# Second layer's attention: value matmuls of two steps issued together, every second step

## The chip, the cores and the metric

The kernel runs on one core of one Trainium2 chip. The metric is the device time of one launch in microseconds (us). Five engines work side by side from instruction queues of their own and meet through semaphores: TensorE (PE in the profile; its weight loads are PEld), VectorE (DVE), ScalarE (ACT), GpSimd (POOL) and SyncE (SP, which here only issues DMAs).

## The reference, cut to what matters

Two layers of attention and feed-forward work on 2048 tokens of width 128. The change touches only the last block, an attention with 8 heads in which each head's query, key and value come from five experts with gates:

```
q5 = (x @ Wq).reshape(b, t, H, E, DH)             # H=8, E=5, DH=64
kv = (x @ Wkv).reshape(b, t, 2, H, E, DH)
q = einsum('bthed,bthe->bhtd', q5, sd_g)          # gates: the top 3 of 5 experts
k = einsum('bthed,bthe->bhtd', k5, ss_g)
v = einsum('bthed,bthe->bhtd', v5, ss_g)
attn = softmax(einsum('bhid,bhjd->bhij', q * scale, k))
out = einsum('bhij,bhjd->bihd', attn, v)
o5 = einsum('bthd,dm->bthm', out, Wo)...; x + einsum('bthem,bthe->btm', o5, md)
```

## The kernel before

Everything stays in on-chip memory. The last block goes through 8 heads (`h`), each through 4 chunks (`c`) of 512 queries, each chunk through `M1` = 8 steps of 256 keys: 32 steps (`U1`) a head, 256 in all, numbered `u`. One list, `SEQ1`, sets the order of work on every engine: `merge` puts a step's foreground (`foreground1`) between background items (`preparation1`) that have due times in steps, and each engine walks the list and does its own part of each item. For a step `u` the foreground items are:

- `S`: the scores of step `u`, 4 full-width matmuls on PE (L775, L776) into two of four PSUM banks; ACT then takes their exponential (L960) into one of five buffers `pbuf1`.
- `V` (L786): the value product of a step, on PE, for the step two before. Each of two key tiles of 128 gives 64 output rows; the first tile uses columns 0 to 63 of the array and the second 64 to 127 (`tile_position=(0, 64 * i)`). Both add up in PSUM bank `ACC`. Each fp32 matmul is two records in the trace, so a `V` has four.
- `D`: the running denominator of that same step, an addition of the exponentials, the first 704 of 1024 columns on DVE (L1280 the first time, L1283 after that), the rest on POOL (L1383).
- `O`: every 8 steps ACT copies the sum out of `ACC`; `F`: two steps after it PE folds the two halves and sums the denominators (L797, L802), DVE divides (L1291, L1292), POOL applies the expert mask and adds into `z` (L1394, L1398).

The background, for the head that comes next, is `proj` (48 a head, three fp32 matmuls each, L747 to L749, read by DVE with the gates at L1238 and summed over the experts by POOL), `t` and `q2` (transposes, L581, read by ACT), and `max` (64 a head, one matmul of 512 columns, L759, read by a row maximum on DVE, L1256). A cast of the next head's weights (`w`, L1230 and L1231, on DVE) comes once a head.

All results of `proj`, `max`, `t`, `q2` and `F` go through a ring of three PSUM banks. In PE's code, `take` waits until the reader of the item three turns earlier in the ring is done:

```
turn = ring.turn[step]
if turn >= len(RING):
    wait_read(pe, ring, ring.order[turn - len(RING)])
return ring.bank(step)
```

The foreground of the second half of a step, before the change:

```
if 0 <= u - 2 < U1 * H1:
    seq += [("V", u - 2), ("D", u - 2)]
```

Within a head, steps 2 to 19 carry the `proj` items (2 or 3 a step, with about 2 `max`); steps 20 to 31 and 0 to 1 carry `max` (1 to 3 a step) and the last transposes. The last head has no `proj`.

Of the kernel before, what the change touches and what calls it, by code (L numbers as in the profile page):

```python
# [32 lines left out]
D = 128  # L33
# [125 lines left out]
def build(nc, A):  # L159
    ctx = ExitStack()  # L160
    with ctx:
# [211 lines left out]
        def foreground1(u, half):  # L373
            if half == 0:
                return [("S", u)] if u < U1 * H1 else []
            seq = []
            if 0 <= u - 2 < U1 * H1:
                seq += [("V", u - 2), ("D", u - 2)]
                if (u - 1) % M1 == 0:
                    seq.append(("O", (u - 1) // M1 - 1))  # L380
            if 0 <= u - 4 < U1 * H1 and (u - 3) % M1 == 0:
                seq.append(("F", (u - 3) // M1 - 1))
            return seq
# [6 lines left out]
        for c in range(NC):  # L390
            u = 2 * (N0 * (NG - 1) + LAST0[c] + 3) + 1
# [9 lines left out]
        for n in range(NT):  # L401
            u = U1 * (H1 - 1) + M1 * (n // TPC + 1) + 3
# [6 lines left out]
        assert [s for s in SEQ0 if s[0] in ("pj", "mix")] == [  # L409
            ({"sd": "pj", "sd2": "mix"}[s[0]], s[1]) for s in NORM if s[0] != "sd3"]  # L410
        SEQ1 = merge(by_place(preparation1() + after1), U1 * H1 + 16, foreground1)
        ring0 = Ring(SEQ0, ("max", "F", "pj", "mix", "lin"), ("k", "q", "q2", "at", "lt", "lt2"))
        ring1 = Ring(SEQ1, ("proj", "max", "F", "y"), ("t", "q2", "zt"))
# [1033 lines left out]
```

## Time and profile before

| what | value |
| --- | --- |
| median of 3 runs | 1856.27 us (1856.07 to 1857.29) |
| profiled execution, span | 1857.2 us |
| PE busy | 1645.3 us, 89% |
| DVE busy | 1435.4 us, 77% |
| POOL busy | 878.0 us, 47% |
| ACT busy | 782.5 us, 42% |

The only time shown of the profiled execution is its span, from its first to its last instruction. It lies 0.9 us over the median of the runs, so what lies around the span is taken as nothing. The 256 steps of the last block run from 796.6 us to about 1833 us of it. "Busy" of PE is the union of the matmul records; a record lasts longer than the time until the next one can start, so gaps are best read from the starts.

### The profile page before, as it was taken

The page shows a single profiled execution, that of the slowest core. Times are in us where ns is not written, and L with a number is a line of the kernel's source. Part 1 is how long each engine was busy: PE and PEld are TensorE (multiplying, and loading weights), DVE is VectorE, ACT ScalarE, POOL GpSimd, SP SyncE. Part 2 cuts the span into 40 slices and gives each one's busy share as a digit, 9 for nine tenths or more (in the row PEclk, how much of TensorE's full clock was granted, in tenths as well). Part 3 has the DMA queues.
Part 4 walks back from the last instruction along what each step waited for, and adds up shares of the span by engine and source line. Part 5 has one row for each costly group of instructions (what it writes and reads, how often), then busy time and mean ns, then how long its engine had stood idle before and what let it go on. Part 6 is the DMA issues. An engine that isn't in the chain of part 4 may idle for free.

```text
span 1857.2 us, 26270 instructions
## 1 busy us (share of the span) xinstructions
PE 1645.3 (89%) x8612; PEld 999.3 (54%) x8612; DVE 1435.4 (77%) x2387; ACT 782.5 (42%) x1046; POOL 878.0 (47%) x906
## 2 busy tenths in 40 slices
PE   3899999999999672699899899899999899899997
PEld 2555555555554361566466466466565565565554
DVE  4996785785786369888888888888898888988862
ACT  3457557567556320223433434334334234234441
POOL 2710000000000024358678589589588587687654
PEclk9799999999999775889899999999999999999996
DMA  2000000000000000000000000000000000000000
GB/s 58 1 1 1 1 1 1 1 1 1 1 1 1 11 1 11 0 11 1 11 1 2 11 1 1 11 1 1 12 1 1 11 1 1 1 1 1 1 11 13
DMA packets 12224, 9.34 MB, mean 5 GB/s; under 512 B 3840, under 2 KB 11584, under 8 KB 12096
## 3 DMA queue, kind: packets, MB, share of 16 engines
q1 hardware_dynamic: 12096, 7.66, 1.5%
q8 instruction: 77, 1.26, 0.3%
q14 instruction: 51, 0.42, 0.1%
HBM read 6.61 MB, written 1.05 MB: 4 GB/s over the span
## 4 chain that ended last, share of the span: by engine, by line
PE 66%; DVE 19%; issue 7%; POOL 5%; ACT 2%; SPq 0%; DMA 0%; DVEq 0%; POOLq 0%; ACTq 0%
PE ps L786 10%; PE ps L606 8%; PE ps L623 7%; PE ps L638 7%; PE ps L759 6%; PE ps L581 5%; PE ps L775 4%; PE ps L776 4%; DVE den L1283 3%; PE ps L747 3%; DVE mxp L1256 3%; PE ps L749 2%; PE ps L748 2%; POOL z L1398 2%; PE ps L797 2%
## 5 line engine op out<-in xcount | busy, mean ns | idle before, releaser
L960 ACT ACTIVATE pbuf<-ps 128x1024 f32<-128x1024 f32 x256 | 262.1, 1024 | 524.0 <-PE ps L776 520.9
L1074 DVE TENSOR_REDUCE mxp<-ps 128x1 f32<-128x512 f32 (+3 forms) x560 | 354.2, 671 | 112.2 <-PE ps L606 56.2
L1256 DVE TENSOR_REDUCE mxp<-ps 128x1 f32<-128x512 f32 x512 | 342.5, 682 | 66.8 <-PE ps L759 66.1
L875 ACT ACTIVATE pbuf<-ps 128x1024 f32<-128x1024 f32 (+3 forms) x320 | 281.7, 896 | 199.1 <-PE ps L626 98.5
L1283 DVE TENSOR_TENSOR den<-den,pbuf 128x704 f32<-128x704 f32 x224 | 292.0, 1303 | 1.1
L786 PE MATMUL ps<-pbuf,h_v 128*64 128x512 f32 x1024 | 284.4, 634 | 0.0
L759 PE MATMUL ps<-k1T,q1T 128*128 128x512 f32 x512 | 223.4, 453 | 38.7 <-DVE mxp L1256 25.1
L1383 POOL TENSOR_TENSOR den<-den,pbuf 128x320 f32<-128x320 f32 x224 | 235.0, 1049 | 42.1 <-ACT pbuf L960 26.5
L606 PE MATMUL ps<-kM,qT 128*128 128x512 f32 (+3 forms) x640 | 243.6, 427 | 9.5 <-ACT kM L862 4.3
L1238 DVE TENSOR_TENSOR gt<-ps,gate 128x320 f32<-128x320 f32 x384 | 182.6, 484 | 54.8 <-PE ps L749 51.7
L623 PE MATMUL ps<-qT,kM 128*128 128x512 f32 (+3 forms) x640 | 207.7, 399 | 8.4 <-ACT pbuf L875 8.4
L775 PE MATMUL ps<-q1T,k1T 128*128 128x512 f32 x512 | 209.4, 409 | 2.3 <-ACT q2T L950 2.3
L776 PE MATMUL ps<-q2T,k2T 65*128 65x512 f32 x512 | 204.6, 400 | 0.0
L606 PEld LDWEIGHTS ps<-kM,qT 128*128 128x128 f32 x640 | 122.4, 197 | 118.7 <-DVE mxp L1074 88.7
L747 PE MATMUL ps<-wh,xh 128*128 128x320 f32 x384 | 136.1, 355 | 53.5 <-DVE gt L1238 36.9
L1367 POOL TENSOR_TENSOR gs<-gt 128x384 f32<-128x384 f32 x120 | 148.3, 1236 | 67.0 <-DVE gt L1238 65.3
L759 PEld LDWEIGHTS ps<-k1T,q1T 128*128 128x128 f32 x512 | 98.8, 194 | 146.3 <-DVE mxp L1256 87.0
L638 PE MATMUL ps<-pbuf,stagev 128*32 128x512 f32 (+3 forms) x1280 | 152.0, 547 | 0.0
L747 PEld LDWEIGHTS ps<-wh,xh 128*128 128x128 f32 x384 | 73.5, 191 | 142.1 <-DVE gt L1238 68.7
L1325 POOL TENSOR_SCALAR rstd<-meanvar 128x4 f32<-128x4 f32 x12 | 2.7, 227 | 304.5 <-DVE meanvar L995 304.5
L1340 POOL COPY stagev<-qkv 128x512 f32<-128x512 f32 x4 | 2.9, 722 | 288.8 <-PE ps L638 266.1
L623 PEld LDWEIGHTS ps<-qT,kM 128*128 128x128 f32 x640 | 117.9, 195 | 35.4 <-ACT pbuf L875 22.9
(212 smaller groups left out, 2484.3 us busy)
## 6 DMA issues: line engine op xcount, KB each, us to landing
wraw<-in_Wkv SPq DMA_DIRECT2D x16, 160.0 KB, 2.6
wraw<-in_Wq SPq DMA_DIRECT2D x8, 160.0 KB, 2.3
out<-x SPq DMA_DIRECT2D x4, 256.0 KB, 2.3
wqkv<-in_wqkvT SPq DMA_DIRECT2D x1, 192.0 KB, 4.0
masks<-in_masks SPq DMA_DIRECT2D x1, 128.0 KB, 4.1
dft<-in_dft SPq DMA_DIRECT2D x1, 128.0 KB, 2.3
wout<-in_Wo SPq DMA_DIRECT2D x2, 64.0 KB, 2.6
ident<-in_ident SPq DMA_DIRECT2D x1, 64.0 KB, 5.7
```

What stands on the lines that cost most here:

```text
L606: mm = pe.matmul(ps[:, bank, w * a:w * (a + 1)], qT[:, g % 2, P * it:P * (it + 1)], kM[g % 2][:, h + a, CH * b:CH * b + w], start=True, st ...
L623: mm = pe.matmul(ps[:, b, off:CH], kM[g % 2][:, h, P * jt:P * (jt + 1)], qT[:, g % 2, CH * c + off:CH * (c + 1)], start=True, stop=jt < TP ...
L638: mm = pe.matmul(ps[32 * h:32 * h + 32, ACC, off:CH], stagev[:, g % 2, jt, h, :], pbuf0[:, u % NP0, h % 2, off:CH], start=jt == 0, stop=jt ...
L747: pe.matmul(o, xh[:, t], wh[:, j, :], start=True, stop=False)
L759: pe.matmul(ps[:, bank, :], q1T[:, h % 2, P * it:P * (it + 1)], k1T[:, h % 2, CH * b:CH * (b + 1)], start=True, stop=True).then_inc(s_turn ...
L775: pe.matmul(ps[:, b, :], k1T[:, h % 2, t], q1T[:, h % 2, q], start=True, stop=False)
L776: mm = pe.matmul(ps[:, b, :], k2T[0:D1 + 1, h % 2, t], q2T[0:D1 + 1, h % 2, q], start=False, stop=True)
L786: mm = pe.matmul(ps[64 * i:64 * i + 64, ACC, :], h_v[:, h % 2, 2 * m + i, :], pbuf1[:, u % NP1, i, :], start=m == 0, stop=m == M1 - 1, til ...
L875: nc.scalar.activation(pbuf0[:, u % NP0, :, off:CH], ps[:, b:b + 2, off:CH], ACT.Exp, scale=float(D0) ** -0.5).then_inc(s_exp, 1)
L1074: v.tensor_reduce(mxp[:, i, h:h + n, b], ps[:, ring0.bank(step), 0:w * n].rearrange("p (h k) -> p h k", h=n), AX.X, ALU.max).then_inc(s_re ...
L1256: v.tensor_reduce(mxp1[:, it % TPC, b:b + 1], ps[:, ring1.bank(step), :], AX.X, ALU.max).then_inc(s_read1d, 1)
L1283: v.tensor_tensor(dn, dn, w, ALU.add).then_inc(s_den1, 1)
```

## The change

The `V` of an even step is no longer issued two steps later, but together with that of the following odd step: in every odd step `u`, `V` of `u - 3` and `V` of `u - 2` stand one behind the other. In even steps only `D` stands there. `D`, `O` and `F` keep their places.

```
@@ -375,7 +375,9 @@
                 return [("S", u)] if u < U1 * H1 else []
             seq = []
             if 0 <= u - 2 < U1 * H1:
-                seq += [("V", u - 2), ("D", u - 2)]
+                if u % 2:
+                    seq += [("V", u - 3), ("V", u - 2)]
+                seq.append(("D", u - 2))
                 if (u - 1) % M1 == 0:
                     seq.append(("O", (u - 1) // M1 - 1))
             if 0 <= u - 4 < U1 * H1 and (u - 3) % M1 == 0:
```

Lines after it stand two higher than before (L786 is L788, L759 is L761, and so on). The order of work changes on PE alone.

First place, PE in step 112 of 256 (head 3, the 17th of its 32 steps, one with `proj`), from the `max` before `V` to the start of step 113. L747 to L749 are `proj`, L759 is `max`, L775 and L776 are `S`. Before:

```order
L759 MATMUL ps<-k1T,q1T 128x512
L786 MATMUL ps<-pbuf,h_v 64x512 x2
L747 MATMUL ps<-wh,xh 128x320
L748 MATMUL ps<-wl,xh 128x320
L749 MATMUL ps<-wh,xl 128x320
L759 MATMUL ps<-k1T,q1T 128x512
L775 MATMUL ps<-q1T,k1T 128x512
L776 MATMUL ps<-q2T,k2T 128x512
```

The same place now:

```order
L761 MATMUL ps<-k1T,q1T 128x512
L749 MATMUL ps<-wh,xh 128x320
L750 MATMUL ps<-wl,xh 128x320
L751 MATMUL ps<-wh,xl 128x320
L761 MATMUL ps<-k1T,q1T 128x512
L777 MATMUL ps<-q1T,k1T 128x512
L778 MATMUL ps<-q2T,k2T 128x512
```

The even step has lost its `V`; four ring items follow each other with only PE's own work between them.

Second place, PE in steps 124 and 125 (head 3, around the weight cast of DVE), from the first `max` of step 124 to the last of step 125. Before:

```order
L759 MATMUL ps<-k1T,q1T 128x512 x2
L786 MATMUL ps<-pbuf,h_v 64x512 x2
L759 MATMUL ps<-k1T,q1T 128x512
L775 MATMUL ps<-q1T,k1T 128x512
L776 MATMUL ps<-q2T,k2T 128x512
L775 MATMUL ps<-q1T,k1T 128x512
L776 MATMUL ps<-q2T,k2T 128x512
L759 MATMUL ps<-k1T,q1T 128x512 x2
L786 MATMUL ps<-pbuf,h_v 64x512 x2
L759 MATMUL ps<-k1T,q1T 128x512
```

The same place now:

```order
L761 MATMUL ps<-k1T,q1T 128x512 x3
L777 MATMUL ps<-q1T,k1T 128x512
L778 MATMUL ps<-q2T,k2T 128x512
L777 MATMUL ps<-q1T,k1T 128x512
L778 MATMUL ps<-q2T,k2T 128x512
L761 MATMUL ps<-k1T,q1T 128x512 x2
L788 MATMUL ps<-pbuf,h_v 64x512 x4
L761 MATMUL ps<-k1T,q1T 128x512
```

The `V` of step 122 has gone from between the `max` items of step 124 to the `V` of step 123, behind the two `max` of step 125.

## Rows read from the trace of the kernel before

**Rows 1.** The page: busy time of each engine; the chain that ended last.

```profile
PE 1645.3 (89%) x8612; PEld 999.3 (54%) x8612; DVE 1435.4 (77%) x2387; ACT 782.5 (42%) x1046; POOL 878.0 (47%) x906
...
PE 66%; DVE 19%; issue 7%; POOL 5%; ACT 2%; SPq 0%; DMA 0%; DVEq 0%; POOLq 0%; ACTq 0%
```

**Rows 2.** The page's costliest groups: value matmuls, and DVE's denominator.

```profile
L1283 DVE TENSOR_TENSOR den<-den,pbuf 128x704 f32<-128x704 f32 x224 | 292.0, 1303 | 1.1
L786 PE MATMUL ps<-pbuf,h_v 128*64 128x512 f32 x1024 | 284.4, 634 | 0.0
```

**Rows 3.** PE's timeline in step 122: start, length, instruction, count.

```profile
1304.82 0.65 PE L786 MATMUL ps<-pbuf,h_v 128*64 128x512 f32 x2
...
1305.30 0.60 PE L786 MATMUL ps<-pbuf,h_v 128*64 128x512 f32 x2
1305.83 0.50 PE L759 MATMUL ps<-k1T,q1T 128*128 128x512 f32 x1
1306.17 0.40 PE L775 MATMUL ps<-q1T,k1T 128*128 128x512 f32 x1
```

**Rows 4.** PE's timeline, steps 112 (from 1266.03) and 113 (from 1269.52), with `proj`.

```profile
1267.41 0.40 PE L759 MATMUL ps<-k1T,q1T 128*128 128x512 f32 x1
1267.74 1.08 PE L786 MATMUL ps<-pbuf,h_v 128*64 128x512 f32 x4
1268.75 0.41 PE L747 MATMUL ps<-wh,xh 128*128 128x320 f32 x1
...
1269.29 0.39 PE L759 MATMUL ps<-k1T,q1T 128*128 128x512 f32 x1
1269.52 0.40 PE L775 MATMUL ps<-q1T,k1T 128*128 128x512 f32 x1
...
1270.91 0.40 PE L759 MATMUL ps<-k1T,q1T 128*128 128x512 f32 x1
1271.15 0.31 PE L747 MATMUL ps<-wh,xh 128*128 128x320 f32 x1
...
1271.68 1.08 PE L786 MATMUL ps<-pbuf,h_v 128*64 128x512 f32 x4
1272.69 0.42 PE L747 MATMUL ps<-wh,xh 128*128 128x320 f32 x1
```

**Rows 5.** DVE's timeline in the same two steps.

```profile
1268.62 1.15 DVE L1283 TENSOR_TENSOR den<-den,pbuf 128x704 f32<-128x704 f32 x1
1269.70 0.48 DVE L1238 TENSOR_TENSOR gt<-ps,gate 128x320 f32<-128x320 f32 x1
1270.10 0.68 DVE L1256 TENSOR_REDUCE mxp<-ps 128x1 f32<-128x512 f32 x1
...
1272.51 0.99 DVE L1283 TENSOR_TENSOR den<-den,pbuf 128x704 f32<-128x704 f32 x1
1273.43 0.49 DVE L1238 TENSOR_TENSOR gt<-ps,gate 128x320 f32<-128x320 f32 x1
```

**Rows 6.** PE's timeline in step 109: a `max` that waits [idle before <-releaser].

```profile
1253.50 0.50 PE L759 MATMUL ps<-k1T,q1T 128*128 128x512 f32 x1 [1.25 <-DVE gt L1238]
```

**Rows 7.** PE's and DVE's timelines in steps 116 and 117, behind the `proj` steps.

```profile
1287.06 0.50 PE L759 MATMUL ps<-k1T,q1T 128*128 128x512 f32 x1
...
1289.24 1.27 DVE L1256 TENSOR_REDUCE mxp<-ps 128x1 f32<-128x512 f32 x2
```

**Rows 8.** PE's timeline in step 125, after DVE's weight cast.

```profile
1318.66 1.21 PE L759 MATMUL ps<-k1T,q1T 128*128 128x512 f32 x2 [3.92 <-DVE mxp L1256]
1319.80 1.98 PE L786 MATMUL ps<-pbuf,h_v 128*64 128x512 f32 x4
1321.70 0.79 PE L759 MATMUL ps<-k1T,q1T 128*128 128x512 f32 x1
```

**Rows 9.** Stretches: us, busy (x) of PE, PEld, DVE, ACT, POOL, PEclk, DMA, GB/s.

```profile
1200.32:1283.91 83.59, 79.60 (x411) 53.87 (x410) 71.17 (x119) 28.62 (x39) 72.07 (x86) 1.00 0.00 1
...
1318.66:1322.29 3.63, 3.53 (x7) 1.17 (x8) 3.63 (x6) 0.00 (x0) 3.10 (x4) 0.62 0.45 135
```

**Rows 10.** L1283 alone: min/median/max ns, first and last start.

```profile
L1283 DVE TENSOR_TENSOR den<-den,pbuf x224: 874/1100/3407, 807.6 to 1832.5; 128x704 f32<-128x704 f32 x112
```

More of the change, by code:

```diff
@@ L377, in foreground1 @@
             if 0 <= u - 2 < U1 * H1:
-                seq += [("V", u - 2), ("D", u - 2)]
+                if u % 2:
+                    seq += [("V", u - 3), ("V", u - 2)]
+                seq.append(("D", u - 2))
                 if (u - 1) % M1 == 0:
```

## The prediction

> **What bounds the kernel now.** The page first: PE is busy 89% of the span, DVE 77%, and two thirds of the chain that ended last run over PE, a fifth over DVE [rows 1]. The value matmuls `V` are the costliest PE group: 284.4 us for 1024 records, four to a step [rows 2]. Then the last block by stretches, since both shares are averages. Over the 18 `proj` steps of head 3, PE is busy 79.6 of 83.6 us and DVE 71.2 [rows 9]: PE leads, but DVE is close behind, and only three PSUM banks lie between them. Then the timelines, read by starts. In the steps without `proj`, PE goes on almost without a gap; in those with it, PE sometimes stands still for a bank that DVE has not read, as before the `max` at 1253.50, 1.25 us [rows 6]. So one question decides: does PE keep what it saves, or does it run into an unread bank and leave DVE dry afterwards?
>
> **What a `V` costs, alone and as the second of two.** Alone: from a `max` to `V` 0.33 us, from `V` to the next matmul 1.01 [rows 4], from that to the one behind it 0.34 [rows 3], where two matmuls of 512 columns that follow each other without a `V` stand 0.23 apart (1269.29 to 1269.52, [rows 4]). A lone `V` therefore adds 0.33 + 1.01 + 0.34 - 2 x 0.23 = 1.22 us. Inside it the second pair of records starts 0.48 after the first (1304.82, 1305.30), but the full-width matmul comes 0.53 after that [rows 3]. No `V` stands directly behind another in this trace. Bounds for a second one: 2 x 0.48 = 0.96 us if it goes on at the inner spacing, 1.22 if nothing is saved. I take 0.96, since the extra is seen only at the edges between half-width and full-width work. **The gain is about 0.25 us for each of 128 pairs, 32 us, where PE is the bound on both sides.**
>
> The Trainium skill, TensorEngine Tiling (Array Packing), Key Properties, says that changing the tiling mode, not just the tile, drains TensorE; the trace's two edges agree, 0.10 us before a `V` and 0.05 + 0.11 after it. Taken alone that rule makes this change a pure gain: its time is the first rival's.
>
> **What the move takes away.** In an even step `V` was also PE's occupation while DVE did `D`, 0.99 to 1.15 us here [rows 5]. `D` stays where it was. Without `V`, PE arrives 1.2 us earlier at all that follows up to the next pair, and each ring item needs the bank of the item three turns before. I worked one pair of steps out, 112 and 113 [rows 4, 5], with PE's spacings and DVE's durations as they are:
>
> - Up to the `max` at 1267.41 nothing changes. The next `proj` starts at 1267.65 instead of 1268.75, its `max` at about 1268.17, `S` of step 113 at 1268.40 instead of 1269.52, the first `proj` of 113 at 1269.34.
> - DVE is no faster: `D` from 1268.62 was keeping it from the `proj` of step 112 anyway, which it reads from 1269.70 to 1270.18, then the `max` from 1270.10 to 1270.78. So PE's `max` of step 113 waits for the first bank until 1270.24 (by spacing it could go at 1269.78), and the second `proj` for the second bank, until 1270.84. PE wanted them at 1270.91 and 1271.15 before. The 1.2 us have shrunk to 0.3.
> - 0.53 later the pair starts (1271.37) and takes 0.96 + 1.01: the next `proj` starts at 1273.34. It was 1272.69. PE is **0.65 us later**.
> - DVE read that `proj` 0.74 after its start, at 1273.43, right behind its `D` (1272.51 to 1273.50). Now it is ready for it at the same time and gets it at 1274.08. Nothing pays the loss back: DVE has no ring item during the pair of `V`, and PE none to give it.
>
> **The sum**, in classes of pairs:
>
> 1. *Pairs in `proj` steps*, 9 a head in the first seven heads, 63. Bounds: -0.25 us if no bank binds; +0.96 where DVE already set the start of the odd step's `V`, as at 1253.50 [rows 6], since there the even step's `V` ran in time that PE would have waited. The hand-worked pair gives +0.65. Where DVE is behind at the pair's end, part of it is hidden, so I take +0.50: 63 x 0.50 = +31.5 us.
> 2. *Pairs in steps with `max` alone*: the other 65 but six (next item), 59. In the seven at steps 22 and 23, `q2` waits for a row maximum of DVE, and I count 0. The other 52 have room in the ring: -0.25 each, -13.0 us.
> 3. *The weight cast*, six heads. DVE casts for 6 us, the ring is full, and PE stands 3.92 us before the `max` at 1318.66 [rows 8]. The `V` before that wait ran free of cost; now it runs behind it. There the granted clock is 0.62 over 3.63 us [rows 9], part of it at the lower level of 1.2 GHz, and a `V` takes 1.90 us (1319.80 to 1321.70, [rows 8]) instead of 1.01. Bounds 0.96 and 1.90; I take 1.4, as the clock comes back during the second: 6 x 1.4 = +8.4 us.
> 4. *Paid back*: where `proj` ends, DVE is behind on its own account: the `max` at 1287.06 is read at 1289.24, 2.2 us after its start [rows 7], where a waiting DVE takes it at once. Lateness of PE up to about 1.3 us is then hidden: 7 x -1.3 = -9.1 us.
> 5. ScalarE's exponentials and the copy `O` have at least as much time as before, `F` comes at most behind the later end of the pair and is in item 1, POOL's part of `D` is unmoved and PE doesn't wait for it. The last `V` is issued where it was. Nothing for these.
>
> 31.5 - 13.0 + 8.4 - 9.1 = **+17.8 us**. The profiled execution's own span, 1857.2, becomes 1875.0; against the median of the runs, 0.9 lower, 1874.
>
> **The rivals.**
>
> *Faster: only the edges count.* PE keeps 0.25 us in all pairs but the six at the cast: 122 x -0.25 = -30.5, with +8.4, gives 1834 us. For it: two thirds of the chain are PE, and DVE has 12.4 us idle in those 83.6 [rows 1, 9]. Against it: the banks of step 113 come free at 1270.18 and 1270.78 by DVE's own rows, 0.7 and 0.4 before PE wanted them, and PE now wants them 1.2 earlier. It decides at the mean price of a `proj` pair: under +0.22 us the total is no loss, and with room of over 1.2 us in the ring this rival holds whole. The skill's tiling rule, above, stands for this case. Chance 0.18.
>
> *Nothing that can be told.* DVE's `D` takes 874 ns at best, 1100 in the middle and up to 3407 [rows 10], long where it overlaps POOL's additions. If, at another spacing, those overlaps become shorter by about 0.3 us a pair in 63 pairs, item 1 falls by 18 us, and the result is 1856. The rows show the spread, not which way it moves. Chance 0.12.
>
> *The pair saves nothing on PE.* If the second `V` costs 1.22 us like the first, items 1 and 2 are each 0.25 dearer: 115 x 0.25 = +29, 1903 us. The 0.48 inside a `V` speaks against it. Chance 0.10.
>
> *The forecast*, a `proj` pair costing between 0.3 and 0.8 us: 0.60.
>
> **How the numbers follow.** The likeliest case gives 1874. Without item 1 the sum is 1842.6, so with a price between 0.05 and 0.82 us for a `proj` pair the time lies between 1846 and 1894; that is the range. It leaves out most of the first rival and half of the third, 0.2 in all. A measurement of this kernel can tell 0.2% (3.7 us) from no change. Slower by more than that: the forecast and the third rival, 0.70. Within it: 0.12. Faster: 0.18.
>
> **What the profile of the changed kernel would show.** The second `V` of a pair starts 0.96 us behind the first, and a pair takes 1.97 to the next matmul; 2.2 would refute the saving. In steps 112 and 113 the `proj` behind the pair starts about 7.3 us after `S` of step 112, where it was 6.7, and the idle time of PE before L761 and L749 that DVE ends grows by 4 to 8 us a head. DVE waits longer for PE behind each pair. Two steps with `max` alone get 0.25 shorter, so the last head gets about 3 us shorter while heads 0 to 5 get about 3 us longer each. The wait at the cast grows from 3.9 to about 5.1 us. I am wrong if the `proj` steps keep their length: then DVE's reading was not what held the banks.

## The result, and the profile after

The changed kernel takes **1909.4 us** (median of 4 runs, 1898.8 to 1912.4) where the kernel before takes 1856.3: ratio **1.0274**, 95% interval 1.0245 to 1.0303. The direction was forecast; the size was +17.8 us and is +53.1, outside the range.

The page of the changed kernel (busy time; PE's granted clock in 40 slices; the chain; five of its groups) against [rows 1, 2]:

```profile
PE 1656.8 (87%) x8612; PEld 1023.4 (54%) x8612; DVE 1426.5 (75%) x2387; ACT 781.0 (41%) x1046; POOL 874.3 (46%) x906
...
PEclk9899999999999767799999999999999899899997
...
PE 65%; DVE 21%; issue 9%; ACT 2%; POOL 2%; SPq 0%; DMA 0%; DVEq 0%; ACTq 0%; POOLq 0%
...
L1285 DVE TENSOR_TENSOR den<-den,pbuf 128x704 f32<-128x704 f32 x224 | 278.7, 1244 | 1.1
L761 PE MATMUL ps<-k1T,q1T 128*128 128x512 f32 x512 | 223.0, 466 | 62.6 <-DVE mxp L1258 38.7
L788 PE MATMUL ps<-pbuf,h_v 128*64 128x512 f32 x1024 | 273.6, 659 | 0.0
L1240 DVE TENSOR_TENSOR gt<-ps,gate 128x320 f32<-128x320 f32 x384 | 181.9, 484 | 97.4 <-PE ps L751 97.2
L749 PE MATMUL ps<-wh,xh 128*128 128x320 f32 x384 | 140.5, 366 | 64.0 <-DVE gt L1240 37.2
```

The same two groups, `max` on PE and the read of a `proj` on DVE, in the page of the kernel before:

```profile
L759 PE MATMUL ps<-k1T,q1T 128*128 128x512 f32 x512 | 223.4, 453 | 38.7 <-DVE mxp L1256 25.1
...
L1238 DVE TENSOR_TENSOR gt<-ps,gate 128x320 f32<-128x320 f32 x384 | 182.6, 484 | 54.8 <-PE ps L749 51.7
```

The value matmuls are 10.8 us less busy (284.4 to 273.6). On the other side both engines wait more for each other: PE is idle 62.6 us before `max` instead of 38.7, and DVE 97.4 us before the read of a `proj` instead of 54.8. The ring now runs full and then dry.

First the place worked out, PE's timeline of the changed kernel in steps 112 (`S` starts at 1295.96) and 113, then DVE's, against [rows 4, 5]:

```profile
1298.08 0.50 PE L761 MATMUL ps<-k1T,q1T 128*128 128x512 f32 x1
...
1300.15 0.50 PE L761 MATMUL ps<-k1T,q1T 128*128 128x512 f32 x1 [0.21 <-DVE gt L1240]
1300.75 0.41 PE L749 MATMUL ps<-wh,xh 128*128 128x320 f32 x1
...
1301.38 1.94 PE L788 MATMUL ps<-pbuf,h_v 128*64 128x512 f32 x8
1303.25 0.41 PE L749 MATMUL ps<-wh,xh 128*128 128x320 f32 x1
```

```profile
1302.02 1.12 DVE L1285 TENSOR_TENSOR den<-den,pbuf 128x704 f32<-128x704 f32 x1
1303.99 0.49 DVE L1240 TENSOR_TENSOR gt<-ps,gate 128x320 f32<-128x320 f32 x1 [0.85 <-PE ps L751]
```

Counted from `S` of step 112, the pair of `V` starts after 5.42 us (5.34 was worked out) and the `proj` behind it after 7.29 (7.31; 6.66 in the kernel before). DVE is dry for 0.85 us there. The pair itself takes 1.87 us to the next matmul, not 1.97.

Then a place that was not worked out: steps 100 and 101 (PE, then DVE, then POOL, then a stretch with its granted clock):

```profile
1239.62 0.42 PE L749 MATMUL ps<-wh,xh 128*128 128x320 f32 x1 [2.23 <-DVE mxp L1258]
...
1240.82 3.23 PE L788 MATMUL ps<-pbuf,h_v 128*64 128x512 f32 x8
1243.97 0.42 PE L749 MATMUL ps<-wh,xh 128*128 128x320 f32 x1
```

```profile
1235.78 3.18 DVE L1285 TENSOR_TENSOR den<-den,pbuf 128x704 f32<-128x704 f32 x1
```

```profile
1235.30 2.91 POOL L1400 TENSOR_TENSOR z<-z,onm 128x1280 f32<-128x1280 f32 x1
```

```profile
1239.60:1243.95 4.35, 4.33 (x12) 1.47 (x12) 3.26 (x5) 0.00 (x0) 4.12 (x7) 0.61 0.01 2
```

PE stops 2.23 us for a bank, DVE's `D` takes 3.18 us while POOL's long addition into `z` runs, and behind the stop the granted clock is 0.61, mostly the lower level of 1.2 GHz. The pair of `V`, now behind the stop instead of one `V` on each side of it, takes 3.15 us in place of 1.87. In the kernel before, the same stop was 1.41 us long, and the granted clock stayed at 1.00 over all of its `proj` steps [rows 9]:

```profile
1216.43 0.41 PE L747 MATMUL ps<-wh,xh 128*128 128x320 f32 x1 [1.41 <-DVE mxp L1256]
```

In the changed kernel's profiled execution PE stops 2.08 to 2.24 us in step 5 (second to seventh head) and in step 13 (first to seventh head), and at 11 of these 13 stops the clock fell. Of the 21 stops of 1.1 to 1.5 us in that of the kernel before, one, in the first head, has a fall behind it.

From the starts of `S` in both profiled executions, the length of each pair of steps can be compared. The differences repeat from head to head within 0.1 us, except in the first head and where the clock falls in one execution and not in the other. Summed by the prediction's classes:

| class | forecast, us | measured, us |
| --- | --- | --- |
| 1. 63 pairs in `proj` steps | +31.5 | +56.7 |
| 2. the pairs in `max` steps but steps 22 and 23, and the last head | -13.0 | -13.0 |
| 2. steps 22 and 23, seven heads | 0 | +4.1 |
| 3. weight cast, six heads | +8.4 | +9.4 |
| 4. paid back behind the `proj` steps | -9.1 | none to be seen |

The agreement of the second row is partly chance: steps 24 and 25 gave 0.7 us a head instead of 0.25 (2.3 in the first head, where the clock fell in the kernel before and not in the changed one), while steps 30 and 31, behind the cast, lost 1.7 us in all and the last head gave 1.9 instead of 4. The measured column adds up to 57.1 us; the end of the kernel gives some of it back (the spans differ by 53.4). Within class 1, averages over seven heads of the nine pairs of steps from 2 and 3 to 18 and 19 are +0.20, +2.46, +1.22, +0.41, -1.07, +2.18, +1.12, +0.64 and +0.94. Steps 4 and 5 and steps 12 and 13, the two pairs of `proj` steps in which DVE's `D` meets POOL's addition into `z`, stand out.

### The profile page after: what moved, and what is told of

Read it like the earlier page. It is cut to its first block, busy times and chain, and to the rows that moved or that the text cites. A ratio compares the mean times of both kernels' runs of the same rounds, so it can differ in the third digit from the quotient of the medians.

```text
span 1910.6 us, 26270 instructions
## 1 busy us (share of the span) xinstructions
PE 1656.8 (87%) x8612; PEld 1023.4 (54%) x8612; DVE 1426.5 (75%) x2387; ACT 781.0 (41%) x1046; POOL 874.3 (46%) x906
## 4 chain that ended last, share of the span: by engine, by line
PE 65%; DVE 21%; issue 9%; ACT 2%; POOL 2%; SPq 0%; DMA 0%; DVEq 0%; ACTq 0%; POOLq 0%
PE ps L788 12%; PE ps L608 8%; PE ps L625 6%; PE ps L640 6%; PE ps L761 5%; PE ps L583 4%; DVE mxp L1258 4%; PE ps L777 4%; PE ps L778 4%; PE ps L749 3%; DVE den L1285 3%; DVE gt L1240 2%; PE ps L751 2%; PE ps L750 2%; DVE mxp L1076 2%
## 5 line engine op out<-in xcount | busy, mean ns | idle before, releaser
L1285 DVE TENSOR_TENSOR den<-den,pbuf 128x704 f32<-128x704 f32 x224 | 278.7, 1244 | 1.1
L761 PE MATMUL ps<-k1T,q1T 128*128 128x512 f32 x512 | 223.0, 466 | 62.6 <-DVE mxp L1258 38.7
L788 PE MATMUL ps<-pbuf,h_v 128*64 128x512 f32 x1024 | 273.6, 659 | 0.0
L1240 DVE TENSOR_TENSOR gt<-ps,gate 128x320 f32<-128x320 f32 x384 | 181.9, 484 | 97.4 <-PE ps L751 97.2
L1385 POOL TENSOR_TENSOR den<-den,pbuf 128x320 f32<-128x320 f32 x224 | 224.8, 1004 | 43.3 <-ACT pbuf L962 27.6
L749 PE MATMUL ps<-wh,xh 128*128 128x320 f32 x384 | 140.5, 366 | 64.0 <-DVE gt L1240 37.2
L1369 POOL TENSOR_TENSOR gs<-gt 128x384 f32<-128x384 f32 x120 | 139.0, 1158 | 122.4 <-DVE gt L1240 120.8
L761 PEld LDWEIGHTS ps<-k1T,q1T 128*128 128x128 f32 x512 | 101.2, 199 | 142.5 <-DVE mxp L1258 72.0
L749 PEld LDWEIGHTS ps<-wh,xh 128*128 128x128 f32 x384 | 75.1, 195 | 138.2 <-DVE gt L1240 46.1
```

The costliest lines, as they stand in the source:

```text
L749: pe.matmul(o, xh[:, t], wh[:, j, :], start=True, stop=False)
L761: pe.matmul(ps[:, bank, :], q1T[:, h % 2, P * it:P * (it + 1)], k1T[:, h % 2, CH * b:CH * (b + 1)], start=True, stop=True).then_inc(s_turn ...
L788: mm = pe.matmul(ps[64 * i:64 * i + 64, ACC, :], h_v[:, h % 2, 2 * m + i, :], pbuf1[:, u % NP1, i, :], start=m == 0, stop=m == M1 - 1, til ...
L1285: v.tensor_tensor(dn, dn, w, ALU.add).then_inc(s_den1, 1)
```

## Which part of the change costs: four partial versions

Theory at this point: a pair of `V` saves PE time wherever the ring has room; in the `proj` steps DVE has not read the banks, and PE's longer stops bring the clock down. Rivals: pairing costs wherever it is done, or all of it is the weight cast, or PE's order itself is at fault and not DVE. All versions below replace the same lines. This is the form with a condition; `paired(w)` is true for the odd steps that take both `V`:

```
+                if u % 2 and paired(u):
+                    seq.append(("V", u - 3))
+                if u % 2 or not paired(u + 1):
+                    seq.append(("V", u - 2))
                 seq.append(("D", u - 2))
```

The runs came from four chips; the kernel before, run beside each group, has medians of 1855.0 (these four versions), 1854.5, 1855.2 and 1857.9 us, so the ratios compare better than the times.

**Pairs only in `max` steps**: `paired = w > U1 * (H1 - 1) + 2 or w % U1 in (1, 21, 25, 27, 31)`.

> Pairs only where no `proj` stands: 51 pairs (steps 1, 21, 25, 27, 31 of each head and all of the last head); elsewhere V as before. The theory (a pair saves PE about 0.34 us where the ring has room; the loss comes from the steps with `proj` and from the low clock that PE's stops bring) expects 51 x -0.34 = -17 us, about 1839 us, and the low-clock stretches of before (seven short ones between 800 and 1800 us) unchanged. The rival, that pairing itself costs time wherever it is done, expects over 1860.

1855.7 us, ratio 0.9992 (0.9968 to 1.0017): the gain that was expected did not come. The step lengths say why. Steps 0 and 1, 26 and 27 and nearly all of the last head are 0.34 us shorter a pair, as in the change, but steps 30 and 31, right behind the weight cast, are 0.75 longer: the low clock after the cast lasts 6.8 us there instead of 3.4. One head (the fifth) lost 3 us more to a fall of the clock at its step 5. So pairing is not a loss in itself, and the clock had to be counted here as well.

**Pairs only in `proj` steps**: `paired = w < U1 * (H1 - 1) and 3 <= w % U1 <= 19`.

> Pairs only in the steps with `proj`, 63 of them. The theory expects the whole loss of the change and more, since the gain of the other steps is gone: the comparison of step lengths gives about +8.6 us a head for seven heads, +60, less 0 to 10 for what later steps recover: 1905 to 1920 us. The rival, that the loss sits mostly at the weight cast, expects under 1870.

1914.4 us, ratio 1.031 (1.0268 to 1.0352). The whole loss is here; the other steps only gave some back.

**All pairs but those at the cast**: `paired = not (w < U1 * (H1 - 2) and w % U1 == 29)`.

> All pairs but the six behind the weight cast. The price that the step lengths give for a cast pair is 1.9 us and 3.4 us more at the low clock each: the theory expects 6 to 12 us less than the change, 1897 to 1903 us. If the clock at the cast were what makes the change slow, under 1880.

1903.6 us, ratio 1.0251 (1.0209 to 1.0293). That is 6 us less than the change, but the runs of the change alone spread over 13 us, so the times tell no more than that the cast is not the main part. The step lengths tell it better: without these pairs, steps 28 and 29 are within about 0.2 us of the kernel before again, where the change has +9.4 us in the six heads. Item 3 was of the right size and is no explanation of the miss.

**`D` moved with `V`**, in all pairs:

```
+                if u % 2:
+                    seq += [("D", u - 3), ("D", u - 2)]
```

> All 128 pairs, and D moved in the same way: D of both steps stands beside the pair of V, none in the even steps. The theory (without V, DVE's D in the even step keeps the banks from being read, and behind the pair DVE runs dry) expects this to give the loss back: DVE reads the ring in even steps and has two D, about 2 us, while PE does the two V, 1.9 us. 128 x -0.34 = -44 us and up to +11 at the six weight casts: 1815 to 1835 us. The rival, that the loss is in PE's own order or that the clock falls whatever DVE does, expects over 1880.

1875.4 us, ratio 1.0105 (1.0061 to 1.0149): 34 of the 53 us come back, which speaks against the rival (over 1880), but not the 74 to 94 that were expected. Steps 4 and 5 and steps 12 and 13 now are 1.7 and 1.5 us *shorter* than before the change; steps 14 and 15 (+2.8 or more from the second head on), 22 and 23 (+1.4) and the cast pay for it. Moving `D` shifts the fullest place of the ring; it doesn't remove it. A third engine comes in there: in steps 14 and 15 DVE now waits 0.70 us for POOL, in all seven heads, which it does neither before nor with the change (rows below, with the last versions).

## Is it the clock? Useless work in the stops

The change, with 8 matmuls without use added where PE stops in steps 5 and 13. They write into the score banks that the next `S` overwrites:

```
+                    if h < H1 - 1 and u % U1 in (5, 13):
+                        pe.wait_ge(s_exp1, u)
+                        for _i in range(8):
+                            pe.matmul(ps[:, 2 * ((u + 1) % NS), :], k1T[:, h % 2, t], q1T[:, h % 2, q],
+                                      start=True, stop=True)
```

> The change, and 8 further full-width matmuls after S in steps 5 and 13 of the first seven heads, written into the score banks that S of the next step overwrites: work without use, put where PE stops for DVE. They are 14 x 8 x 0.235 = 26 us of PE work. If the low clock behind those two stops is what makes the two pairs cost 2.4 us where they cost 0.8 with the clock up, the low stretches behind them vanish and the kernel gets faster with more work: 14 x -1.6 = -22 us, 1880 to 1893. If the clock has no part, it stays at 1909 or gets up to 26 us slower.

**1888.3 us**, 21 us less than the change with 26 us more work on PE; ratio to before 1.018 (1.0151 to 1.021). PE's timeline in step 101, and the stretch that answers to the one above:

```profile
1228.22 2.00 PE L787 MATMUL ps<-q1T,k1T 128*128 128x512 f32 x8
1230.63 0.41 PE L752 MATMUL ps<-wh,xh 128*128 128x320 f32 x1 [0.41 <-DVE mxp L1266]
...
1231.50 1.94 PE L796 MATMUL ps<-pbuf,h_v 128*64 128x512 f32 x8
1233.37 0.42 PE L752 MATMUL ps<-wh,xh 128*128 128x320 f32 x1
```

```profile
1230.99:1234.58 3.59, 3.59 (x19) 1.89 (x18) 3.37 (x6) 0.00 (x0) 3.51 (x5) 1.00 0.01 2
```

The real matmul still waits for the same bank, but the granted clock stays at 1.00 and the pair takes 1.87 us. From the second head on, steps 4 and 5 and steps 12 and 13 cost +0.86 us each instead of about 2.4.

The control is the same filler in the order of before (`V` of every step in its own step):

> Control of the filler: the order of before, with the same 8 useless matmuls in steps 5 and 13. There PE stops 1.4 and 1.3 us and the clock stays up, so there is no clock to win: 14 x (1.9 - 1.3) = up to +8 us, 1856 to 1864. If the filler made this kernel faster too, it would do something other than hold the clock.

1854.8 us, ratio 0.998 (0.9952 to 1.0007): no difference. Where the clock does not fall, the filler buys nothing, and it fits into the stops. So the clock is about 20 us of the 53: 21 by the medians and by the step lengths of class 1, 17 by the ratios to the kernel before.

## Is it DVE's reading? Less work for DVE in both orders

The kernels of this section leave part of the computation out, the same part in each order, so only the difference of two such kernels counts. The first two cut DVE's addition in `D` from 704 to 64 columns (the other columns of the denominators keep the first step's value):

```
-                        v.tensor_tensor(dn, dn, w, ALU.add).then_inc(s_den1, 1)
+                        v.tensor_tensor(dn[:, 0:64], dn[:, 0:64], w[:, 0:64], ALU.add).then_inc(s_den1, 1)
```

> The order of before, with DVE's D additions cut to 64 of 704 columns (columns 64 to 703 of the denominators keep their first step's value: part of the sum is left out). DVE loses about 1.2 us a step. Expected 1780 to 1835 us: the stops before steps 5 and 13 go. Serves as the base of the next kernel.

> The order of the change with the same short D (the same part of the denominators is left out). If DVE's D in the even steps is what keeps the banks from being read, the change turns into a gain: 0.34 us a pair in most of the 128, 20 to 40 us less than the kernel before it. If the loss is in PE's order itself (the four ring items in a row, whatever DVE has to do), it is again 20 us or more slower than that kernel.

1825.0 us in the order of before, 1854.4 in that of the change: still 29 us slower, where 20 to 40 faster was expected if `D` were the whole cause. DVE's `D` alone in the second kernel (min/median/max ns) shows what was wrong with the expectation:

```profile
L1288 DVE TENSOR_TENSOR den<-den,pbuf x224: 208/325/2879, 806.6 to 1826.9; 128x64 f32<-128x64 f32 x112
```

Eleven times less data, and the longest still takes 2.9 us. So the next two also made `D` a copy of 64 columns, and let the row maximum read 128 of its 512 (the rest of the maxima is left out):

```
-                        v.tensor_tensor(dn, dn, w, ALU.add).then_inc(s_den1, 1)
+                        v.tensor_copy(dn[:, 0:64], w[:, 0:64]).then_inc(s_den1, 1)
...
-                    v.tensor_reduce(mxp1[:, it % TPC, b:b + 1], ps[:, ring1.bank(step), :],
+                    v.tensor_reduce(mxp1[:, it % TPC, b:b + 1], ps[:, ring1.bank(step), 0:128],
```

> The order of before with DVE made nearly free: D after the first is a copy of 64 columns, and the row maximum reads 128 of 512 columns (the rest of the denominators and of the maxima is left out). DVE loses some 2.3 us a step. PE bound alone: below the 1825 us of the kernel with the short D. Base of the next kernel.

> The order of the change with the same nearly free DVE (the same parts are left out). If all of the loss comes from the banks that DVE has not yet read, every pair now saves PE about 0.34 us: 30 to 44 us less than the kernel before it. If it is still slower than that, PE's order or another engine costs it.

1804.2 and 1813.7 us: the order of the change is now 9.5 us slower. Four of the nine `proj` pairs (steps 2, 6, 8 and 16) have turned into gains of 0.15 to 0.2 us. Steps 10 and 11 are even, steps 14 and 15 and steps 18 and 19 still cost 0.65 and 0.36, and steps 4 and 5 and steps 12 and 13 0.84 us each (2.5 where the clock falls). Step 100 of the second of these, DVE and then POOL:

```profile
1195.59 2.65 DVE L1288 COPY den<-pbuf 128x64 f32<-128x64 f32 x1
```

```profile
1195.27 2.92 POOL L1403 TENSOR_TENSOR z<-z,onm 128x1280 f32<-128x1280 f32 x1
```

A copy of 64 columns, 0.18 us when alone, starts inside POOL's addition and ends when that ends (1198.24 and 1198.19). DVE is held, whatever the size of `D`. It is so wherever `D` starts inside that addition, 25 times in each kernel: with its 704 columns (before and after the change) `D` ends 0.75 us after the addition, and as this copy 0.05 us after it. What DVE reads from PSUM is not held. In step 116 of the kernel before, a row maximum inside the addition takes its usual 0.69 us, and the `D` behind it 2.56 (DVE, then POOL):

```profile
1286.15 0.69 DVE L1256 TENSOR_REDUCE mxp<-ps 128x1 f32<-128x512 f32 x1 [0.17 <-PE ps L759]
1286.76 2.56 DVE L1283 TENSOR_TENSOR den<-den,pbuf 128x704 f32<-128x704 f32 x1
```

```profile
1285.64 2.92 POOL L1398 TENSOR_TENSOR z<-z,onm 128x1280 f32<-128x1280 f32 x1
```

The last two kernels keep these cuts and shorten POOL's two operations on the head's output to one of four token tiles (the rest of the output is left out):

```
+                    zs = slice(tiles.start, tiles.start + 1)
-                    g_.tensor_tensor(z[:, tiles], z[:, tiles], onm[:], ALU.add).then_inc(s_z, 1)
+                    g_.tensor_tensor(z[:, zs], z[:, zs], onm[:, 0:1], ALU.add).then_inc(s_z, 1)
```

(and the same for the product into `onm` ahead of it).

> The order of before, DVE nearly free as in the pair of kernels before, and POOL's onm and z operations cut to one of four token tiles (three quarters of the head's output beside the rest are left out). Expected a little under 1804. Base of the next kernel.

> The order of the change with the same cuts. If the +0.84 us (2.5 with the clock down) that remained at steps 4 to 5 and 12 to 13 comes from DVE's D, which does not end before POOL's 2.9 us addition into z ends, both go to -0.17 as in the other `proj` pairs and the kernel is 14 to 22 us less than before with the same cuts by this alone, so 5 to 13 us faster where the last pair of kernels was 9.5 slower. If POOL has no part, it is 9.5 slower again.

**1759.3 and 1751.5 us: the change is now 7.8 us faster** (four runs each, 1757.7 to 1760.3 and 1750.3 to 1752.0, no overlap). Both places went to -0.15 us. The same step in the second kernel, DVE and POOL:

```profile
1166.10 0.18 DVE L1288 COPY den<-pbuf 128x64 f32<-128x64 f32 x1
```

```profile
1164.16 0.87 POOL L1404 TENSOR_TENSOR z<-z,onm 128x320 f32<-128x320 f32 x1
1165.11 1.02 POOL L1372 TENSOR_TENSOR gs<-gt 128x384 f32<-128x384 f32 x1
```

So PE's new order doesn't lose time by itself; it loses it on the work of DVE and POOL. It doesn't gain in the `proj` steps either: five of the nine pairs give 0.14 to 0.18 us, but steps 6, 14 and 18 cost 0.25, 0.45 and 0.35, so the nine come to +0.2 us a head, and the 7.8 us are those of the `max` steps and the last head. In step 110 (steps 14 and 15 of head 3) PE still waits for DVE there, 0.89 us where the order of before waits 0.25; DVE's other work on the ring was not cut. The weight cast keeps its price, +0.87 us a head: that is the second `V`, moved behind a stop, at the full clock.

Shortening POOL's two operations took 45 us off the order of before as well (1804.2 to 1759.3), more than any other single cut here. What it does without the cuts on DVE, and what a complete but divided addition into `z` would give, was not run.

## A version that beats both

**Pairs where they paid**: `paired = w % U1 in (1, 21, 27) or (w > U1 * (H1 - 1) + 2 and w % U1 not in (7, 15, 23))`.

> V paired only at steps 1, 21 and 27 of each head and at 12 of 16 places of the last head, picked by the step lengths of the first runs (steps 25 and 31, beside the weight cast, are out: there the low clock lasted 6.8 us and not 3.4). The theory expects 7 x (0.34 + 0.16 + 0.34) + 12 x 0.34 = 10 us less than before and low-clock stretches as before: ratio 0.995. If single pairs only shift the loss to the next stop, 1.000.

1848.7 us, ratio 0.9955 (0.9929 to 0.998), as expected. Two versions put `D` of steps 4 and 12 out of the way of POOL's addition on top of it, with `V` paired there and without:

> The selected pairs of V, and at steps 5 and 13 of the first seven heads V and D both paired (D of the even step, which POOL's long addition into z would hold, goes to the odd step). The step lengths of the run with D beside every pair gave -1.65 and -1.5 us there: 14 x -1.5 = -21 and the selected -8: 1826 us if nothing is given back in the steps behind. If the steps behind give it back (they got 0.6 and 2.8 longer in that run), about 1850.

> The selected pairs of V, and at steps 5 and 13 only D is moved to the odd step while V stays in the even one. DVE reads the ring in the even step and PE keeps its V there: the 1.4 and 1.25 us of stop before the items of steps 5 and 13 should go. Expected -1.3 x 14 = -18 on top of the selected pairs' -8: about 1830 us, and nothing slower than 1849.

1849.3 us (0.9967, 0.9956 to 0.9978) and 1849.8 us (0.9964, 0.995 to 0.9977): nothing on top of the selected pairs. Steps 4 and 5 and steps 12 and 13 are 1.5 to 1.7 us shorter in both, as expected, and the steps behind give most of it back: +0.7 or +0.8 in steps 6 and 7, +1.7 or +1.8 in steps 14 and 15. About 1 us a head is left of it. It is lost again where the clock falls in steps 24 and 25 or 30 and 31 of some heads (1.5 to 2.0 us each), and in the end of the kernel, whose length differs by up to 4 us between executions. For steps 14 and 15 the second of these kernels shows who is behind. Step 110, DVE and then PE:

```profile
1251.92 0.49 DVE L1247 TENSOR_TENSOR gt<-ps,gate 128x320 f32<-128x320 f32 x1 [0.70 <-POOL h_v L1379]
```

```profile
1252.47 0.42 PE L756 MATMUL ps<-wh,xh 128*128 128x320 f32 x1 [0.90 <-DVE gt L1247]
```

The product of DVE's read goes into one of two buffers `gt`, so DVE waits until POOL has summed what stood there, and POOL works without a pause behind its addition into `z`. This wait of 0.70 us stands in steps 14 and 15 of all seven heads in the three versions that move `D`, and not in the selected pairs alone. All three engines are near their limit in the `proj` steps, and a stop removed at one place comes back at the next.

**Selected pairs, and filler at the weight cast** (`if h < H1 - 2 and u % U1 == 29`, 16 matmuls):

> The selected pairs, and 16 useless matmuls (3.8 us) after S in step 29 of the six heads with a weight cast, in PE's stop of 3.9 us. The low clock behind the stop costs a V 0.9 us and the other matmuls of 3.6 us about as much: 6 x -1.8 = -11 us on top of the selected pairs' -8: about 1837 us. If the stop is shorter than the filler and DVE is the bound behind the cast anyway, 1848.

**1845.5 us, ratio 0.9903** (0.9866 to 0.9939), the fastest complete kernel of this study by a little. PE in step 125, against [rows 8], and the granted clock of a long stretch:

```profile
1309.08 3.85 PE L787 MATMUL ps<-q1T,k1T 128*128 128x512 f32 x16
1313.24 1.10 PE L764 MATMUL ps<-k1T,q1T 128*128 128x512 f32 x2 [0.31 <-DVE mxp L1266]
1314.28 1.08 PE L796 MATMUL ps<-pbuf,h_v 128*64 128x512 f32 x4
1315.73 0.50 PE L764 MATMUL ps<-k1T,q1T 128*128 128x512 f32 x1 [0.38 <-DVE mxp L1266]
```

```profile
800.00:1800.00 1000.00, 953.74 (x4632) 604.39 (x4632) 846.52 (x1280) 381.68 (x498) 753.92 (x790) 1.00 0.01 4
```

The clock is 1.00 over 1000 us, where the kernel before has 0.99 and the changed one 0.95. The four records of `V` take 1.08 us again instead of 1.98. Against the selected pairs alone, steps 28 to 31 are 1.7 us a head shorter in all six heads, which is the 1.8 us of the expectation. The time of 1845.5 lies over the expected 1837 in part because the kernel before takes 1857.9 us on this chip: by the ratios the filler gives 10 us, as expected, though the two intervals overlap a little. The other branch, no gain because DVE is the bound behind its cast, did not come: DVE ends two waits of PE there, but of only 0.31 and 0.38 us. A matmul without use is a poor thing to ship; work that is due anyway would be the better filler.

## Why the prediction was wrong in size

**Right.** The question was the right one, and the hand-worked pair came out within 0.1 us at each point. The saving on PE is real and somewhat larger than said: 0.34 us a pair between `max` steps, since the second `V` costs 0.87 us and not 0.96; between `proj` matmuls it is 0.15 to 0.2. That the weight cast would cost 8.4 us (9.4), and that the `max` steps would give 13.0, held. The wait at the cast grew to 5.12 us, as forecast (5.1). The -13.0 of item 2 is partly luck, as said with the table. The first rival, "only the edges count", did not come true even with DVE's and POOL's work cut: the kernel gained 7.8 us there, not 22. The third rival fell with the 1.87 us.

The tiling rule of the Trainium skill named with the prediction (TensorEngine Tiling (Array Packing), Key Properties) agrees with the trace here too: one visit to the half-width mode with eight records takes 1.87 us, two visits with four each 2.02 and one more set of edges. It told the sign of this term and not that of the sum.

**Wrong.** The step that failed is item 1, the price of a pair in the `proj` steps: +0.50 each, taken below the worked value of +0.65. It measured +0.90. With the filler the same pairs cost +0.57 on average, close to the item as written; the rest is the clock. Item 1 reckoned the even step's `V` behind a stop at its price at full clock ("+0.96 where DVE already set the start"). The place quoted for it, step 109, is one of those behind which the clock then fell: the stop was 1.25 us before the change and is 2.08 after. The clock was counted at the cast alone, where the trace of before showed it low. But that trace has one more stop, near the end of the last head, and it is of 2.01 us (PE, then the stretch behind it):

```profile
1820.02 0.52 PE L810 MATMUL ps<-ident,z 128*128 128x128 f32 x3 [2.01 <-POOL z L1398]
```

```profile
1820.02:1825.02 5.00, 5.00 (x16) 2.52 (x18) 1.97 (x2) 1.81 (x5) 4.43 (x5) 0.62 0.00 2
```

The granted clock was 1.00 in the 8 us up to the end of this stop and 0.62 in the 5 us behind it. So the trace of before did show what a stop of 2 us may bring, and the range should have had a case for it. The filler run gives its size: 14 pairs x 1.3 to 1.6 = 18 to 22 us. The step lengths exceed the sum by 39 us (57.1 against 17.8): 21 are this clock, 9 item 4, 4 steps 22 and 23, and 5 the rest of items 1 and 3.

The second failure is item 4, -9.1 us paid back. DVE's backlog at 1289.24 [rows 7] had come from one long `D` beside POOL's addition into `z` (the 2.56 us above), not from a lag that the whole stretch carried along. Pairs in the `proj` steps alone (the second partial version) leave steps 20 to 23 unchanged within 0.1 us, so no part of it appeared; steps 22 and 23, counted at 0, cost 0.6 us each instead. The rival built on DVE's spread [rows 10] looked at the right thing ("long where it overlaps POOL's additions"), but put it among the accidents, where it is bound to two places in every head.

**Open.** POOL's 0.70 us are not the whole price of steps 14 and 15 when `D` moves, and no run tests them alone. Nor is it known where the clock falls or doesn't from launch to launch. The runs of the changed kernel spread over 13 us, their mean granted clock from 0.944 (1898.8 us) to 0.932 (1912.4), while those of before stay within 1.2 us on that chip. On the other chips the kernel before spreads too, up to 27 us: 1852.5 (clock 0.949) to 1879.5 (0.940).

## What to carry to other kernels

Work that is "only PE's" may be what gives the reader of a short ring its time: before bunching it, walk one period, with the bank releases fixed at the reader's times. Where that walk makes a stop longer, price it twice, at full clock and at half clock behind it. And a save at one place of a balanced pair of engines is worth nothing until the next place is read too.

## What the runs showed of the hardware

- GpSimd's long addition between on-chip buffers held VectorE's additions and copies between such buffers until it ended: a 64-column copy took 2.65 us beside a 2.92 us addition and 0.18 us alone. VectorE's reads from PSUM inside the same additions took what they always take (0.69 us for a row maximum).
- Useless matmuls in stops of 2.1 to 2.2 us took 21 us off a kernel of 1909 us; the clock behind the stop stayed at 1.00 instead of 0.61. In stops of 1.3 to 1.4 us, which had left the clock up, they changed nothing.
- A change between full-width and half-width work costs time (0.10 us before a `V`, 0.16 behind it [rows 3, 4]), and eight half-width records in a row pay that once: 0.34 us a pair between 512-column matmuls.
